# The second normalisation of a two-layer kernel in groups of four tiles, with its first rows and constants loaded during the experts

## The reference, cut to what matters

```python
x = L0_attn_x                                  # (4, 1024, 256), float32
xn = _layernorm(x)
s = L0_attn(xn)                                # first layer
g = _silu(L0_ffn(xn))                          # shared part + 16 experts; each takes 128 tokens of each sequence
x = x + s * g
xn = _layernorm(x)                             # second normalisation, x = what follows "x2" below
s = L1_attn(xn)                                # again (xn - mu) / sqrt(var + 1e-05) * gamma + beta, then
                                               # 16 heads of 64, rotary positions, causal softmax, projection
g = _silu(L1_ffn(xn))                          # 8 experts, top 2 of xn @ Wr.T + br + biases for each token
return x + s * g
```

## Time and profile before

| | us |
|---|---|
| median of 3 runs | 2752.32 |
| lowest, highest | 2749.39, 2756.25 |
| the profiled execution | 2745.85 |
| its span | 2744.0 |
| TensorE busy | 2491.4 (91%) |
| VectorE, ScalarE, GpSimd busy | 1303.8, 1131.6, 545.8 |

### The profile page before, as it was taken

The page is one execution under the profiler, slowest core; times in us unless marked ns, Lnnn a source line. Parts: engine busy times, 40 slices in busy tenths (PEclk is TensorE's granted clock), DMA queues, the critical chain, the costliest instruction groups (busy, mean ns, idle before and its releaser), DMA issues. The chain is left out here.

```text
span 2744.0 us, 45828 instructions
## 1 busy us (share of the span) xinstructions
PE 2491.4 (91%) x14626; PEld 1727.1 (63%) x14627; DVE 1303.8 (48%) x3165; ACT 1131.6 (41%) x2597; POOL 545.8 (20%) x487
## 2 busy tenths in 40 slices
PE   6999996999974599999999999999999986999992
PEld 5454544555543466666666666666666656999992
DVE  5455451212114455665665556556566541333335
ACT  3112211111113356666666666666666652222221
POOL 3000002444422133332111111111111110111114
PEclk9999998999995599999999999999999997999996
DMA  5011103876424433222111121112211107666695
GB/s 196 16 38 38 39 22 116 265 220 168 113 46 126 139 101 105 87 91 78 34 43 38 52 55 38 41 35 54 62 31 46 33 24 267 241 235 243 233 350 196
DMA packets 146334, 298.79 MB, mean 109 GB/s; under 512 B 16720, under 2 KB 104800, under 8 KB 135648
## 3 DMA queue, kind: packets, MB, share of 16 engines
q1 hardware_dynamic: 125280, 254.96, 28.7%
q0 software_dynamic: 20992, 43.07, 6.1%
HBM read 196.13 MB, written 68.30 MB: 96 GB/s over the span
## 5 line engine op out<-in xcount | busy, mean ns | idle before, releaser
L1347 DVE CUSTOM_DVE_ANT_0 at_p<-at_ps,atk_mask 128x640 f32<-128x640 f32 (+7 forms) x512 | 375.7, 753 | 259.0 <-PE at_ps L1210 147.1
L1257 ACT ACTIVATE at_p<-at_p,at_nmax 128x640 f32<-128x640 f32 (+7 forms) x512 | 391.6, 769 | 59.5 <-DVE at_nmax L1347 59.5
L1264 ACT ACTIVATE at_pT<-at_ps 128x512 f32<-128x512 f32 (+1 forms) x640 | 325.5, 554 | 202.3 <-PE at_ps L1210 202.0
L1289 POOL TENSOR_TENSOR at_qkT<-at_raw,at_swapped 128x1024 f32<-128x1024 f32 x64 | 150.6, 2353 | 1026.2 <-DVE at_swapped L1362 1026.2
L1210 PEld LDWEIGHTS at_ps<-atk_ident,at_p 128*128 128x128 f32 x2304 | 255.5, 141 | 137.9 <-issue 127.7
L1377 DVE SCALAR_TENSOR_TENSOR at_y<-at_ps,at_inv,at_y 128x256 f32<-128x256 f32 x512 | 215.1, 477 | 222.8 <-PE at_ps L1231 204.1
L1210 PE MATMUL at_ps<-atk_ident,at_p 128*128 128x128 f32 x2304 | 314.9, 278 | 2.0 <-ACT at_p L1257 2.0
L1200 PE MATMUL at_ps<-at_qkT 64*128 64x512 f32 (+3 forms) x1536 | 293.3, 501 | 6.8 <-POOL at_qkT L1289 3.7
L1221 PE MATMUL at_ps<-at_pT,at_v 128*64 128x256 f32 (+1 forms) x2560 | 277.9, 363 | 0.0
L1499 PEld LDWEIGHTS moe_ps<-moe_xT,moe_w 128*128 128x128 f32 x2304 | 271.1, 193 | 5.2 <-ACT moe_xT L1532 1.6
L1499 PE MATMUL moe_ps<-moe_xT,moe_w 128*128 128x128 f32 x2304 | 271.8, 277 | 0.9 <-ACT moe_xT L1532 0.9
(11 more groups left out here) (203 smaller groups left out, 3142.7 us busy)
## 6 DMA issues: line engine op xcount, KB each, us to landing
moe_w<-in_w_w SPq DMA_DIRECT2D x72, 1028.0 KB, 4.8
at_swapped<-at_raw SPq DMA_DIRECT2D x256, 128.0 KB, 2.3
atk_w<-in_w_qkv SPq DMA_DIRECT2D x32, 384.0 KB, 3.1
slot_in<-ex_zero SPq DMA_DIRECT2D x9, 1032.0 KB, 9.6
moe_xs<-slot_in SPq DMA_DIRECT2D x72, 129.0 KB, 2.1
xn_n<-n_stage SPq DMA_DIRECT2D x8, 1024.0 KB, 4.6
ex_wg<-in_w_eg SPq DMA_DIRECT2D x16, 512.0 KB, 3.3
ex_wu<-in_w_eu SPq DMA_DIRECT2D x16, 512.0 KB, 4.8
```

The source lines that it names most:

```text
L1257: act.activation(buf, buf, ACT.Exp, bias=nmax[:, unit:unit + 1], scale=-1.0, accum_out=rsum[:, unit:unit + 1]).then_inc(exp_done, 1)
L1264: act.activation(dst, ring[RING_BANK[part][ev]][:, 0:(i1 - i0) * P].rearrange("p (k c) -> p k c", c=P), ACT.Copy).then_inc(t_read, 1)
L1289: pool.tensor_tensor(out=qkT[x][:, :].rearrange("p (m t) -> p m t", m=2)[:, :, half * CH:(half + 1) * CH], in0=raw[half][:, :].rearrange(" ...
L1347: dve.tensor_tensor_reduce(out=p[unit % LAG][:, 0:(n[0] + 1) * P], in0=scores(*n), in1=mask[:, T - (n[0] + 1) * P:T], scale=-1.0, scalar=3 ...
```

## The change

A new function `renormalize` takes the place of `normalize(nc, "n1", d, False)`. It works on eight groups g of four tiles (512 rows). Its rows of z have four buffers, held outside the stage, and those of groups 0 to 3 are loaded by SyncE at the end of `experts`: groups 0 and 1 when the last expert's adding write of sequence 0 has landed, 2 and 3 when that of sequence 1 has. GpSimd no longer waits for the adding writes at the end of `experts`; those of sequences 2 and 3 are waited for by SyncE inside the new stage, before groups 4 and 6 are loaded. The result tile of the odd experts and the list of rows move into the outer scope, as they are still read then. Eight constants become tiles of the outer scope, loaded through the list `others` (which grows from 15 to 23 entries, still two per expert); attention's identity matrix serves for the transposes. `turned` and `scaled` get two buffers each, half as wide. The order of the steps within the loops of TensorE and ScalarE is another. The router is unchanged.

```diff
@@ experts, SyncE
                 sp.wait_ge(d.n1_x_in, 16 * B + ONE)
                 sp.wait_ge(d.n1_s_in, 16 * B + ONE)
+                for g in range(4):
+                    if g % 2 == 0:
+                        sp.wait_ge(d.n1_late[g // 2], 16)
+                    sp.dma_start(tiles(d.n1_z[g][:, :]), rows_of(d.z, g)).then_inc(d.n1_z_in[g], 16)
@@ experts, GpSimd
-                                                compute_op=ALU.add).then_inc(scattered[u], 16)
+                                                compute_op=ALU.add).then_inc(d.n1_late[b] if e == last else scattered[u], 16)
...
-                for u in range(2):
-                    pool.wait_ge(scattered[u], 16 * B * HE)
@@ build
+                d.n1_z = [n.sb(f"z{g}", TC * C) for g in range(4)]
+                d.ex_eo, d.ex_rows = n.sb("eo", B * C), n.sb("rows", E0 * B, I32)
...
+                d.at_loads += [(dst, src) for dst, (name, cols, src) in zip(d.n1_consts, given)]
...
-                normalize(nc, "n1", d, False)
+                renormalize(nc, d)
@@ renormalize (new), SyncE
+                for g in range(G):
+                    u = g % 2
+                    sp.wait_ge(x_added, g + 1 + ONE)
+                    sp.dma_start(rows_of(d.x2, g), tiles(part(x, g))).then_inc(x2_out, 16)
+                    if g + 4 < G:
+                        if g % 2 == 0:
+                            sp.wait_ge(d.n1_late[(g + 4) // 2], 16)
+                        sp.dma_start(tiles(zg[g % 4][:, :]), rows_of(d.z, g + 4)).then_inc(d.n1_z_in[g % 4], 16)
+                    sp.wait_ge(stage_made, g + 1 + ONE)
+                    sp.dma_start(rows_of(d.xn["n1"], g), tiles(stage[u][:, :])).then_inc(xn_out[u], 16)
+                    if g >= G // B:
+                        sp.wait_ge(scaled_read, 2 * g + 2 + ONE)
+                        for c in range(KC):
+                            sp.dma_start(d.hT1[...], tall[u][...]).then_inc(h_out[u], 16)
@@ renormalize, VectorE
+                for g in range(G):
+                    add_moe(g)
+                    statistics(g)
+                    if g > 0:
+                        staged(g - 1)
+                staged(G - 1)
+                dve.wait_ge(log_ps, G + ONE)
@@ renormalize, TensorE
+                def logits(g):
+                    pe.wait_ge(stage_read, 2 * g + 2 + ONE)
...
+                def turn_scaled(g):
+                    pe.wait_ge(scaled_made, g + 1 + ONE)
...
+                for g in range(G):
+                    pe.wait_ge(stage_made, g + 1 + ONE)
+                    turn_stage(g)
+                    if g > 0:
+                        turn_scaled(g - 1)
+                    logits(g)
+                turn_scaled(G - 1)
@@ renormalize, ScalarE
+                def squash(g):
+                    q = g % 4
+                    act.wait_ge(d.n1_z_in[q], 16 * (g // 4 + 1) + ONE)
+                    act.activation(zg[q][:, :], zg[q][:, :], ACT.Silu).then_inc(squashed, 1)
...
+                squash(0)
+                squash(1)
+                for g in range(G):
+                    for c in range(KC):
+                        stage_evicted(g, c)
+                    if g + 2 < G:
+                        squash(g + 2)
+                    rescaled(g)
+                    for c in range(KC):
+                        scaled_evicted(g, c)
```

More of the change, by code:

```diff
@@ L44 @@
 ROW = C + 2
+FULL_TILES = (TOP * N + E1 * (P - 1)) // P
 W1COLS = KC * 2 * H1 + 2 * KH
@@ L771, in experts @@
         ident = s.sb("ident", P)
-        rows = s.sb("rows", E0 * B, I32)
+        rows = d.ex_rows
         xg = [s.sb(f"xg{q}", B * C) for q in range(AHEAD)]
@@ L776, in experts @@
         hid = [s.sb(f"hid{f}", B * CAP) for f in range(KF)]
-        eo = [s.sb(f"eo{u}", B * C) for u in range(2)]
+        eo = [s.sb("eo0", B * C), d.ex_eo]
         zero, spare = s.sb("zero", TB * ROW), s.sb("spare", TB)
@@ L835, in next_spare @@
                     pool.tensor_scalar(col, col, float(TB * P), None, ALU.add).then_inc(zero_made, 1)
+                last = E0 - 1
                 def scatter(e, u, first):
@@ L1642, in build @@
                 d.n1_x, d.n1_s = n.sb("x", NT * C), n.sb("s", NT * C)
-                d.n1_x_in, d.n1_s_in = n.sem("x_in"), n.sem("s_in")
+                d.n1_z = [n.sb(f"z{g}", TC * C) for g in range(4)]
+                d.ex_eo, d.ex_rows = n.sb("eo", B * C), n.sb("rows", E0 * B, I32)
+                d.n1_x_in, d.n1_s_in, d.n1_z_in = n.sem("x_in"), n.sem("s_in"), n.sems("z_in", 4)
+                d.n1_late = n.sems("late", B, software=True)
+                given = (("gate_w", KC * E1, d.gate_w["n1"]), ("gain", KC, d.gain["n1"]), ("off", KC, d.off["n1"]), ("before", P, d.before),
+                         ("br", E1, d.w["br"]), ("bias", E1, d.w["bias"]), ("rank", E1, d.rank), ("tile_no", SLOT_TILES, d.tile_no))
+                d.n1_consts = [n.sb(name, cols) for name, cols, src in given]
+                d.at_loads += [(dst, src) for dst, (name, cols, src) in zip(d.n1_consts, given)]
                 a.start()
```

210 lines of the change are left out of this document (added).

## The result

The changed kernel takes 2760.97 us (median of 18 runs, 2756.5 to 2765.2), the kernel before 2751.29 us beside it (18 runs): ratio 1.0034, 95% interval 1.0026 to 1.0042, so 9.7 us slower. Forecast were 2761.2 us, 8.9 us more than before. The profiled execution took 2758.09 us, its span is 2755.9 us.

The account below looks back on a forecast made before the run. Chains of waits, no full engine, were taken to bound the gap between experts and attention; the router at 928.0 against 919.1 made +8.9 us, 2754.8 from the profiled run and 2761.2 as a median, range 2750 to 2767.

Parts of the forecast that it names:

- the ring: Stage's steady part: both turnings and all four evictions inside the circle, 12.5 us per four tiles, 25 for eight against 20.3.
- Handover: Experts' end to first SiLU: GpSimd's drain of 4.6 us ends at 821.7, SiLU starts at 825.1 instead of 836.65.
- 4: Rival at the handover: drain ends at 824.2 anyway, +11.4 us in all, 2763.7; within the drain-ends case of chance 0.68.
- Filling: First SiLU to first normalised tiles: these are ready at 837.65 instead of 857.56, 19.9 us won so far.
- The root: GpSimd's root of group 0's variance in the filling: 5.45 us in all, from 830.8 to 836.25.
- End: Last groups to the router: router starts at 928.0, where before it was 919.08.
- s(6): End of group 6's normalised rows, in the steady part: forecast at 909.7 us.
- logits(6): TensorE's 16 products for group 6 near the stage's end: half of 6.83 us, done at 918.8.
- first link: First round of the steady part, without rescaled tiles yet: from 837.65 to group 1's normalised rows at 847.2.
- Rival 1: TensorE at full clock in the stage: ring 11.5 us, -1.8 us in all, 2750.5; chance 0.15, wholly or in part.
- Rival 2: Steady part overlaps instead of closing a ring: TensorE bounds at 7.1 us a group, some 21 us won, 2731; chance 0.06.
- Rival 3: Store behind SyncE's new wait lands late and delays staging: at 3 us beyond its room +9 more, 2770; chance 0.06.

Follow-up runs that it names:

- e11: Changed kernel with TensorE's old order alone (transposes, logits, then scaled transposes of the same group), ScalarE keeping the new order: ratio 0.9967.
- e2: Changed kernel with ScalarE emptying the rescaled tiles of group g-1 after SiLU of group g+2 instead of ahead of the unscaled evictions: 2735.91 us, ratio 0.9965.
- e1: Changed kernel with GpSimd's wait for all four adding writes put back at the end of the experts: 2755.4 us, ratio 1.0038.
- e8: Changed kernel with 16 memsets, each waited for, on GpSimd behind the last adding write: 2775.16 us in one execution.
- e9: Changed kernel with SyncE's first four z loads issued only when all four of the last expert's adding writes have landed: 2751.06 us, ratio 1.0023.
- e6: Changed kernel with SiLU running three groups ahead in place of two, nothing else altered: 2735.65 us, ratio 0.9945.
- e3: Changed kernel with both the eviction order of e2 and SiLU three groups ahead as in e6: 2723.12 us, ratio 0.9891.
- e4: Changed kernel, still in groups of four tiles, with the old orders on both TensorE and ScalarE: 2743.47 us, ratio 0.9997.
- e10: e3 with the late z loads of e9: 2717.49 us, ratio 0.9911.
- e12: Kernel before, in batches of eight tiles, with the new handover and SiLU of two batches on ahead of the rescaling on ScalarE: 2722.6 us, ratio 0.9908.

## Why the prediction was right, step by step

**Ring and end.** The step on which the sign hung was the ring read off the hand-written order: 12.5 us forecast, 12.25 to 12.44 measured (the normalised rows start at 847.11, 859.55, 871.98, 884.23, 896.66 and 909.09). Its links were read right: the earlier trace rows's 9.38 us of VectorE's idling for SiLU are now 6.50 per four tiles. e11 and e2 show the cause and not only the length: break the circle at either engine and 9.6 us are left. The PSUM page of the Trainium skill (PSUM — Partial Sum Buffer, Engine vs sequencer instructions) says the queues of ScalarE, VectorE and GpSimd are strict FIFO. The rows agree: ScalarE stood at L771 until 863.84, though the transposes for L752, behind it, had ended at 862.95 and the first four of them earlier.

**Handover: the step that failed.** "If it is the same 4.6 us, it ends at 821.7": the length was right (e1, e8 and e9), but the drain also can't end before the landings, and the loads of z that the prediction costed at nothing made the last landing 7.7 us instead of 3.8. SiLU came at 827.63, not 825.1: +2.5. The prediction looked at where SyncE's queue stood, not at what its transfers run over. The case was among its rivals (4, the drain ending near 824.2 anyway), priced at the +2.5 that it cost, but with no reason given.

**Filling.** The root took 3.3 us, not 5.45: out of the variance at 833.26, done at 836.56, its first power 1.87 us for four columns where eight took 3.57. Only 1.1 of these 2.1 us were won, as VectorE was at group 1's statistics until 837.6. First normalised rows at 839.02 for 837.65.

**End.** From s(6) = 910.47 to the router 16.9 us, 18.3 forecast. logits(6) took 2.45 us where 3.4 were assumed: part of it at the full clock. Together: +2.5 and -1.1 in handover and filling, about -0.6 in rings and first link, -1.4 at the end: 927.4 for 928.0. Part of the agreement in the total is these errors cancelling. From the stage alone the profiled pair gives +8.3 us, the medians +9.7 with an interval of 7 to 12; the forecast of +8.9 lies between. That 2761.2 met the median within 0.3 us is luck: the kernel before came out at 2751.29 beside it, 1.0 below the 2752.32 that the forecast started from.

**The clock.** Rival 1 held it against the new kernel that its TensorE is idle more often.

```profile
840.00:860.00 20.00, 10.38 (x53) 9.39 (x52) 10.54 (x28) 8.78 (x16) 11.08 (x27) 0.59 0.50 158
860.00:880.00 20.00, 11.82 (x58) 11.09 (x58) 7.04 (x19) 8.79 (x16) 8.32 (x26) 0.59 0.15 53
880.00:900.00 20.00, 9.09 (x49) 8.50 (x49) 11.24 (x30) 6.28 (x13) 6.97 (x22) 0.59 0.49 158
...
854.05 2.08 PE L716 MATMUL n_ps<-ahead_gate_w,n_turned 128*128 128x8 f32 x16 [1.84 <-ACT n_turned L752]
...
866.50 3.58 PE L716 MATMUL n_ps<-ahead_gate_w,n_turned 128*128 128x8 f32 x16 [1.84 <-ACT n_turned L752]
```

It was 0.59 with TensorE busy 9.1 us of 20, where the earlier trace rows have 0.50 with 13.5. Some sets of 16 logits took 2.0 us and some 3.58. So the prediction's clock of 0.5 was wrong for these stretches. The Trainium skill says that activity releases the throttle (TensorE: Matmul & The Clock Gate, What's actually happening); here the stretch with less work had more clock, so busy time in 20 us was a poor guide to it. The clock did little, as the logits are outside the ring of 12.4 us. In e6 they are inside it, and there the spacing followed the clock: 8.9 us with logits of 3.58 (858.75, 875.33), 7.3 to 7.8 with logits of 1.95 to 2.6.

**The others.** Rival 2, a loop that overlaps (about 21 us won), is what e3 is: 38 us less than the changed kernel on the same chip. Its gain was forecast too low, as its 7.1 us a group were TensorE's at the low level. Rival 3, the late store, had no part in the changed kernel (no row has staging idle for `xn`), and appears in e3. The router and what follows took 24.5 us to the attention as before.

**Where the change's gain went.** The handover won 8.6 us (11.1 against 19.6 from issue to SiLU). From SiLU to the router the group size lost 10.0 (e4 against before), TensorE's order 18.4 (after against e11) and ScalarE's order won 11.1 (e11 against e4): 17.3, as measured, each with the 1.6 to 2.7 us of clock named above. Best of these kernels are e3 (0.9891), e10 (0.9911) and, in eights with two edits to the kernel before, e12 (0.9908); their intervals overlap.

## What to carry to other kernels

Write down, for a pipelined stage with orders by hand, the circle from one group's result back to its own engine, and count what stands ahead in each engine's queue: moving one step (TensorE's `turn_scaled(g - 1)` ahead of `logits(g)`) put a set of transposes and two evictions inside it and cost more than the earlier start won. Halving the group only pays if the ring halves with it. When a ring is opened, look again at who waits for whom: in e3 VectorE looked full, but the small operations of GpSimd set its pace. When a load is moved under another transfer, ask whose landing it delays and who waits for that: here it was the barrier.

## What the runs showed of the hardware

GpSimd's drain at the end of a block with indirect DMA writes took 4.627 us in before, e1 and e8, with 0, 0 and 16.7 us of other work behind the last write, and in the eleven kernels without a wait or other work ended 4.6 us behind the last issue or 1.6 to 1.7 us behind the last landing, whichever was later; at the end of the two normalisations it took 0.3 us. An adding write of 128 KB lands in 3.7 to 3.9 us alone and in 7.0 to 8.2 us beside SyncE's z loads. GpSimd's first power of the stage took 3.57 us for 8 columns and 1.87 for 4; later ones took 1.7 to 1.9 us for 8 and 1.0 to 2.0 for 4. Its small operations, 0.20 to 0.24 us elsewhere, took 1.32 (kernel after, at 842.66) and 1.18 us (e3, at 857.62) where they ran beside one of VectorE's additions. TensorE's eight transposes of the staged rows took 1.97 us at the low level and 1.09 at the high one, 16 logits 3.58 and 1.85 to 1.95.
